# Gathering h for a graph attention layer: two tiles per chunk by column copies, and some tiles by single-row transfers

## The reference, cut to what matters

```
h = maximum(layernorm(x), 0)                       # 12500 nodes, 64 features
h_edge = ((h[src] + edge_attr) @ W)                # 200000 edges, sorted by dst, 2 heads of 64
s = leaky_relu(<h_edge, attn_l> + <h @ W, attn_r>[dst])
alpha = softmax of s over the edges of each dst
ft = segment_sum(h_edge * alpha, dst); mean over heads; batch norm; relu; + x
```

## Time and profile before

| | us |
|---|---|
| median of 3 runs (1983.07 to 1984.06) | 1983.39 |
| the profiled execution's own time | 1986.6 |
| span of the profiled execution | 1984.9 |
| POOL busy | 1469.0 (74%), 1558 instructions |
| DVE busy | 1141.2 (57%) |
| ACT busy | 413.0 (21%) |

### The profile page before, as it was taken

The page is one execution under the profiler, slowest core; times in us unless marked ns, Lnnn a source line. Parts: engine busy times, 40 slices in busy tenths (PEclk is TensorE's granted clock), DMA queues, the critical chain, the costliest instruction groups (busy, mean ns, idle before and its releaser), DMA issues.

```text
span 1984.9 us, 25091 instructions
## 1 busy us (share of the span) xinstructions
PE 925.4 (47%) x6252; PEld 662.5 (33%) x6252; DVE 1141.2 (57%) x3283; ACT 413.0 (21%) x2927; POOL 1469.0 (74%) x1558
## 2 busy tenths in 40 slices
PE   3537535433553445344534543554355435543555
PEld 2425323322332233233323332333233223332335
DVE  7878646555655465556545554555455546554665
ACT  3420111311131122112211221122113111211102
POOL 7777777777777777777777777777777777777771
PEclk9758767676676677667766766676667666766676
DMA  8734322232223222322232232223222322232235
GB/s 231 176 81 124 94 59 60 61 92 60 60 67 86 60 60 68 85 60 61 74 79 60 61 81 72 60 61 93 60 60 60 93 60 61 60 92 60 60 69 135
DMA packets 72959, 156.70 MB, mean 79 GB/s; under 512 B 28756, under 2 KB 33376, under 8 KB 66160
## 3 DMA queue, kind: packets, MB, share of 16 engines
q0 software_dynamic: 49536, 52.31, 15.7%
q1 hardware_dynamic: 22162, 99.02, 15.2%
q10 hardware_dynamic: 1112, 3.73, 0.7%
HBM read 143.71 MB, written 9.80 MB: 77 GB/s over the span
## 4 chain that ended last, share of the span: by engine, by line
POOL 68%; issue 22%; DVE 4%; PE 3%; DMA 2%; ACT 0%; ACTq 0%; DVEq 0%; SPq 0%; POOLq 0%
POOL work L681 67%; PE p_s L930 1%; DMA er_run<-er_tab,er_idx 1%; DMA acc<-in_x 1%; DMA h_tab<-acc 1%; PE po L1053 1%; PE pt L919 0%; POOL er_run L695 0%; DVE acc L1534 0%; DVE acc L1230 0%; DVE acc L1228 0%; DVE work L1222 0%; DVE scaled L1220 0%; PE pt L1112 0%; PE p_s L962 0%
## 5 line engine op out<-in xcount | busy, mean ns | idle before, releaser
L681 POOL DMA_INDIRECT work<-h_tab,srcI x1477 | 1398.0, 946 | 450.4 <-issue 450.1
L1178 DVE COPY elh<-work 128x16 f32<-128x16 f32 x196 | 38.7, 198 | 699.8 <-DMA work<-h_tab,srcI 697.8
L990 PE MATMUL p_s<-ident,elh 128*32 128x128 f32 x196 | 50.7, 412 | 746.8 <-DVE elh L1178 746.8
L825 ACT ACTIVATE cols<-acc 32x2 f32 x2688 | 298.9, 201 | 136.3 <-issue 136.3
L1053 PE MATMUL po<-scaled,work 128*65 128x64 f32 x3104 | 250.8, 257 | 77.6 <-issue 74.5
L990 PEld LDWEIGHTS p_s<-ident,elh 128*32 128x32 f32 x196 | 25.7, 155 | 758.0 <-DVE elh L1178 754.1
L1053 PEld LDWEIGHTS po<-scaled,work 128*65 128x65 f32 x3104 | 245.5, 173 | 87.8 <-issue 87.0
L838 ACT ACTIVATE fexp<-fdif 1x2 f32<-1x2 f32 x49 | 9.9, 203 | 1209.3 <-DVEq L1134 1209.3
L962 PE MATMUL p_s<-work,wpair 128*32 128x256 f32 x784 | 234.9, 466 | 14.5 <-DVE p_r L1452 12.9
L952 PE MATMUL pt<-ident,work 128*128 128x128 f32 x784 | 159.4, 356 | 62.2 <-DVE work L1183 61.5
L1534 DVE TENSOR_TENSOR acc<-acc,po 65x64 f32 x776 | 168.4, 217 | 27.7 <-DVE acc L1534 1.4
(11 more groups left out here) (214 smaller groups left out, 968.5 us busy)
## 6 DMA issues: line engine op xcount, KB each, us to landing
work<-in_ea_t SPq DMA_DIRECT2D x49, 1024.0 KB, 6.1
ohT_i<-in_dst_n SPq DMA_DIRECT2D x49, 512.0 KB
work<-h_tab,srcI POOLq DMA_INDIRECT x1477, 2.5
acc<-hT_tab SPq DMA_DIRECT2D x2, 1562.5 KB, 14.0
h_tab<-acc SPq DMA_DIRECT2D x1, 2887.5 KB
work<-in_x SPq DMA_DIRECT2D x1, 2800.0 KB
out<-work SPq DMA_DIRECT2D x5, 448.0 KB
acc<-in_x ACTq DMA_DIRECT2D x3, 672.0 KB
```

The costliest lines, as they stand in the source:

```text
L681: pool.indirect_dma_start(out=row, out_offset=None, in_=x if c < RAW else h_tab, in_offset=bass.IndirectOffsetOnAxis(ap=srcI[:, c, j, g:g ...
L825: copied = nc.scalar.activation(view(cols[0:HALF, n % COL_BUFS, 0, i:i + 1], [[P, H]]), view(acc[CP:P, 0, bass.ds(r, 1)], [[NACC, H]]), AC ...
L990: m = mm(sT_ps[:, j * P:(j + 1) * P], elh[:, c % 2, j, :, :].rearrange("p h g -> p (h g)"), ident[:, :], start=False, stop=True, skip_grou ...
```

## The change: what it does

- **Columns.** Every chunk from 5 to 48 has two column tiles, (0, 12) and (1, 12): 88 tiles in place of 21. Both are made within one `load_cols(c)`, for chunk c + 2. The numbers of the two tiles' nodes are packed into one word, so one register serves two copies: the low 14 bits by `%`, the high ones by `>>`.
- **Who copies.** ACT takes 7 of 8 batches of 16 registers, so 112 registers and 224 copies in a chunk. DVE takes the last 16 registers and 32 copies in a new `load_cols(c)` of its own, between `make_e(c + 1, 2)` and the sums of the other 8 groups.
- **Adding.** `add_cols` treats 256 columns in place of 128, and waits for both `cols_ok` and `cols_dve_ok`.
- **Rows.** `ROW_FIRST` is 6 and every second chunk has a row tile: 21 tiles of 128 rows (chunks 7, 9, ... 47) beside the 64 rows of the last chunk. SP's loop issues two batches of 16 rows before `load_dst(c)` and two after `load_bond(c + 1)`.

In the cut below the first `load_cols`, with `nc.scalar`, is ACT's; the second, with `v.tensor_copy`, is DVE's.

```diff
-ROW_FIRST = NCH - 1
+ROW_FIRST = 6
-BATCHES = (3, 2)
-ROW_SPAN, ROW_SHARE = 8, 5
+BATCHES = (2, 2)
+ROW_SPAN, ROW_SHARE = 2, 1
-COL_FIRST, COL_STEP = 7, 2
+COL_FIRST = 5
-COL_BATCH = 32
+COL_BATCH, COL_ACT = 16, 7
+HI = 14
+LOW = (1 << HI) - 1
 def col_tiles(c):
-    return [(0, COL_G)] if c >= COL_FIRST and (c - COL_FIRST) % COL_STEP == 0 and c < NCH - 1 else []
+    return [(j, COL_G) for j in range(EPP)] if c >= COL_FIRST else []
...
             def load_cols(c):
-                n, part = divmod(c - COL_FIRST + 1 + COL_STEP, COL_STEP)
...
+                n = c + 2 - COL_FIRST
+                if n < 0 or c + 2 >= NCH:
                     return
-                if n >= COL_BUFS and part == 0:
+                if n >= COL_BUFS:
                     act.wait_ge(cols_added, n - COL_BUFS + 1)
-                cc = COL_CHUNKS[n]
-                for r0 in range(part * COL_PART * COL_BATCH, (part + 1) * COL_PART * COL_BATCH, COL_BATCH):
-                    for i, r in enumerate(col_regs(cc, r0, r0 + COL_BATCH, ENG.Activation), r0):
-                        copied = nc.scalar.activation(view(cols[0:HALF, n % COL_BUFS, 0, i:i + 1], [[P, H]]),
-                                                      view(acc[CP:P, 0, bass.ds(r, 1)], [[NACC, H]]), ACT.Copy)
+                for r0 in range(0, COL_ACT * COL_BATCH, COL_BATCH):
+                    for i, r in enumerate(col_regs(c + 2, r0, r0 + COL_BATCH, ENG.Activation), r0):
+                        for to, node in ((i, r % (LOW + 1)), (P + i, r >> HI)):
+                            copied = nc.scalar.activation(view(cols[0:HALF, n % COL_BUFS, 0, to:to + 1], [[GROUP, H]]),
+                                                          view(accf[CP:P, bass.ds(node, 1)], [[NACC, H]]), ACT.Copy)
                     copied.then_inc(cols_ok, 1)
...
             def bond_scores(c):
                 if col_tiles(c):
-                    pe.wait_ge(cols_added, COL_CHUNKS.index(c) + 1)
+                    pe.wait_ge(cols_added, c - COL_FIRST + 1)
...
+            step(v.tensor_scalar(t[:, 0:P], node[:, P:EPP * P], HI, None, ALU.logical_shift_left))
+            step(v.tensor_tensor(node[:, 0:P], node[:, 0:P], t[:, 0:P], ALU.bitwise_or))
             signal(coffs_ok)
...
+            def load_cols(c):
+                n = c + 2 - COL_FIRST
+                if n < 0 or c + 2 >= NCH:
+                    return
...
+                if n >= COL_BUFS:
+                    dve.wait_ge(cols_added, n - COL_BUFS + 1)
+                for i, r in enumerate(col_regs(c + 2, COL_ACT * COL_BATCH, P, ENG.DVE), COL_ACT * COL_BATCH):
+                    for to, node in ((i, r % (LOW + 1)), (P + i, r >> HI)):
+                        copied = v.tensor_copy(view(cols[0:HALF, n % COL_BUFS, 0, to:to + 1], [[GROUP, H]]),
+                                               view(accf[CP:P, bass.ds(node, 1)], [[NACC, H]]))
+                copied.then_inc(cols_dve_ok, 1)
             def add_cols(c):
...
-                dve.wait_ge(cols_ok, (n + 1) * P // COL_BATCH)
+                dve.wait_ge(cols_ok, (n + 1) * COL_ACT)
+                dve.wait_ge(cols_dve_ok, n + 1)
                 step(v.tensor_copy(cols[HALF:F, n % COL_BUFS, 0, :], cols[0:HALF, n % COL_BUFS, 1, :]))
-                at = bt[c % 2][0:F, g // 2, j * P:(j + 1) * P]
+                at = bt[c % 2][0:F, COL_G // 2, :]
                 v.tensor_tensor(at, at, cols[0:F, n % COL_BUFS, 0, :], ALU.add).then_inc(cols_added, 1)
...
+                    if g0 == 0:
+                        load_cols(c)
```

More of the change, by code:

```diff
@@ L52 @@
 ROW_BUFS = 4
-ROW_FIRST = NCH - 1
+ROW_FIRST = 6
 BATCH = 16
-BATCHES = (3, 2)
-ROW_SPAN, ROW_SHARE = 8, 5
+BATCHES = (2, 2)
+ROW_SPAN, ROW_SHARE = 2, 1
 COL_G = 12
-COL_FIRST, COL_STEP = 7, 2
+COL_FIRST = 5
 COL_BUFS = 2
-COL_BATCH = 32
-COL_PART = P // COL_BATCH // COL_STEP
-assert COL_PART * COL_STEP * COL_BATCH == P and COL_G % 2 == 0
+COL_BATCH, COL_ACT = 16, 7
+assert COL_G % 2 == 0 and COL_BATCH * (COL_ACT + 1) == P
+HI = 14
+LOW = (1 << HI) - 1
+assert N <= LOW and LOW < H * NACC
 def col_tiles(c):
-    return [(0, COL_G)] if c >= COL_FIRST and (c - COL_FIRST) % COL_STEP == 0 and c < NCH - 1 else []
-COL_CHUNKS = [c for c in range(NCH) if col_tiles(c)]
+    return [(j, COL_G) for j in range(EPP)] if c >= COL_FIRST else []
 def row_tiles(c):
@@ L157, in gnn_kernel @@
         row_tile = sb("row_tile", [P, ROW_BUFS, FH])
-        cols = sb("cols", [P, 4, H, P])
+        cols = sb("cols", [P, COL_BUFS, H, GROUP])
         raw_mv = sb("raw_mv", [P, 2, EPP, CG])
@@ L321, in gnn_kernel @@
         cols_ok = sem("cols_ok")
+        cols_dve_ok = sem("cols_dve_ok")
         cols_added = sem("cols_added")
@@ L453, in col_regs @@
             return nc.values_load_multi_w_load_instructions(
-                coffs[c:c + 1, o0:o1], engines=[which], min_val=0, max_val=N - 1,
-                skip_runtime_bounds_check_because="src and dst hold numbers of nodes")[1]
+                coffs[c:c + 1, o0:o1], engines=[which], min_val=0, max_val=((N - 1) << HI) + LOW,
+                skip_runtime_bounds_check_because="each half of a word holds the column of a node, in [0, N)")[1]
         h_bytes = h_tab.rearrange("n f -> (n f)").bitcast(u8)
@@ L815, in load_cols @@
             def load_cols(c):
-                n, part = divmod(c - COL_FIRST + 1 + COL_STEP, COL_STEP)
-                if not 0 <= n < len(COL_CHUNKS):
+                n = c + 2 - COL_FIRST
+                if n < 0 or c + 2 >= NCH:
                     return
-                if n >= COL_BUFS and part == 0:
+                if n >= COL_BUFS:
                     act.wait_ge(cols_added, n - COL_BUFS + 1)
-                cc = COL_CHUNKS[n]
-                for r0 in range(part * COL_PART * COL_BATCH, (part + 1) * COL_PART * COL_BATCH, COL_BATCH):
-                    for i, r in enumerate(col_regs(cc, r0, r0 + COL_BATCH, ENG.Activation), r0):
-                        copied = nc.scalar.activation(view(cols[0:HALF, n % COL_BUFS, 0, i:i + 1], [[P, H]]),
-                                                      view(acc[CP:P, 0, bass.ds(r, 1)], [[NACC, H]]), ACT.Copy)
+                for r0 in range(0, COL_ACT * COL_BATCH, COL_BATCH):
[3 more added lines that the diff above has]
+                                                          view(accf[CP:P, bass.ds(node, 1)], [[NACC, H]]), ACT.Copy)
                     copied.then_inc(cols_ok, 1)
@@ L1420, in _ @@
             last_base = []
+            def load_cols(c):
+                n = c + 2 - COL_FIRST
+                if n < 0 or c + 2 >= NCH:
+                    return
+                if n == 0:
+                    dve.wait_ge(cols_table_in, 32)
+                if n >= COL_BUFS:
[5 more added lines that the diff above has]
+                copied.then_inc(cols_dve_ok, 1)
             def add_cols(c):
-                j, g = col_tiles(c)[0]
-                n = COL_CHUNKS.index(c)
+                n = c - COL_FIRST
                 dve.wait_ge(bt_in[c % 2], 16 * (c // 2 + 1))
-                dve.wait_ge(cols_ok, (n + 1) * P // COL_BATCH)
+                dve.wait_ge(cols_ok, (n + 1) * COL_ACT)
+                dve.wait_ge(cols_dve_ok, n + 1)
                 step(v.tensor_copy(cols[HALF:F, n % COL_BUFS, 0, :], cols[0:HALF, n % COL_BUFS, 1, :]))
-                at = bt[c % 2][0:F, g // 2, j * P:(j + 1) * P]
+                at = bt[c % 2][0:F, COL_G // 2, :]
                 v.tensor_tensor(at, at, cols[0:F, n % COL_BUFS, 0, :], ALU.add).then_inc(cols_added, 1)
```

## The result

| | before | after |
|---|---|---|
| median, 4 runs each | 1983.72 (1983.07 to 1984.43) | 2561.62 (2559.69 to 2563.42) |
| span of the profiled execution | 1984.9 | 2558.0 |

The ratio is 1.2915, with a 95% interval of 1.2899 to 1.2932: 29% slower. The forecast of 2700 is 5% too high, the range of 2370 to 2900 holds the time, and the side was right. Measured once more, beside another kernel, the changed kernel gave 1.2918 (1.2897 to 1.294).

A forecast was written before the change was run, and what follows sets the result against it. POOL's count of gathers bounds the kernel now; afterwards ACT's 45.3 us and DVE's 10.2 form a 55.5 us period. 199.9 us, 44 periods (2442) and 60.5 make a span of 2702, given as 2700; range 2370 to 2900.

The forecast's parts named there:

- The ring: From one `pT` to the next, DVE's first part and ACT's copies run one after the other: period 55.5 us.
- POOL: Gathers on POOL: 88 fewer, 1389 left, at 1.251 us each; 36.9 us a chunk, under the new period.
- ACT's stage: ACT's register loads and copies from the start of `pT`: 33.0 us plus 12.3 for taking numbers apart, 45.3 us.
- rest: On ACT, the start behind `pT`, the end of the last copy and stalls: 1.4 us a chunk.
- Unpacking: One `%` or `>>` added to each ACT copy: 0.055 us a copy, 12.3 us a chunk, bounds 0 and 0.12.
- the ring's DVE part: DVE from `add_cols` to `sdif`'s end, without the wait for gathered rows: 10.2 us a chunk.
- Is it hidden?: Added register work on ACT is not hidden: ACT idles 1.96 of a load's 1.98 us, so its queue is not ahead.
- Rival 1: Taking numbers apart on ACT nearly free, 0 to 0.03 us a copy: 2160 to 2455 us; chance 0.18.
- Rival 2: Taking numbers apart on ACT dear, 0.075 to 0.12 us a copy, or more stalls: 2900 to 3340 us; chance 0.12.
- Rival 3: POOL stays the bound, faster: 88 gathers saved, 110.1 us, so 1873; ACT's part at most 26.7 us; chance 0.03.
- Rival 4: SP as new bound: 26.3 us of rows a chunk plus waits; needs a period under about 30; no separate chance.
- DVE's own copies: DVE's 32 copies and their load between `sdif` and the chunk's end: 11.0 us, covered by ACT's 45.3, costing nothing.

The follow-up runs named there:

- opening the ring: Changed kernel with three column buffers in place of two and copies made for chunk c + 3: 2101.03 us, ratio 1.0598.
- row tiles alone: Kernel before with only the change's 21 row tiles and four batches of 16 rows a chunk, column tiles as before: 1956.66 us, ratio 0.9869.
- one column tile: Kernel before with the 21 row tiles and one unpacked column tile a chunk for chunks 5 to 47, copied by ACT: 1929.41 us, ratio 0.9733.
- the ring open and no unpacking: Changed kernel with one register a copy, three column buffers and copies made for chunk c + 3: 2000.86 us, ratio 1.0087.
- The column tiles alone: Changed kernel with the row-tile settings as before, so without its new row tiles: 2555.88 us, ratio 1.2888.
- the run with one register a copy: Changed kernel with numbers left unpacked, loads of 32 registers for 32 copies: 2461.38 us, ratio 1.2416.

## Why the prediction was right, step by step

**Where the bound goes.** Right. The ring of `add_cols`, `sdif`, `pT` and ACT's copies set the pace; the wait, its line and its releaser are as named, and opening the ring gave 461 us back.

**POOL.** Right: 1389 gathers, (1311.7 + 427.7) / 1389 = 1.252 us each, and 88 fewer are worth nothing in this kernel. Where POOL stays the bound, each gather less was worth 1.24 to 1.27 us (row tiles alone: 26.6 us for 21; one column tile: 53.1 for 43).

**ACT's stage**, forecast 45.3 us, measured 41.7:

| term | forecast | measured |
|---|---|---|
| 7 loads of 16 registers | 7.7 | 7 x 1.03 = 7.2 |
| 224 copies with unpacking | 23.9 + 12.3 = 36.2 | 224 x 0.147 = 32.9 |
| rest | 1.4 | 1.6 |

**Unpacking** is the term that was mis-sized: 0.055 us a copy was taken, nearly a whole instruction, and it is 0.040, since the operation rides in the instruction that is there. That is 224 x 0.015 = 3.4 us a chunk too much. The prediction took the value between bounds of 0 and 0.12 without a row that priced it, so being this near is partly luck. With the load's -0.5 and small ones of +0.2 and +0.3 (the ring's DVE part is 10.5, forecast 10.2) the period is 52.23 in place of 55.5, and 44 x 3.3 = 145 us is the whole miss of the span, forecast 2702: 200.3 + 44 x 52.23 + 59.5 = 2558.

**Is it hidden?** No, as argued. The engine still idles 1.02 of the 1.03 us of a load, so the queue is not ahead. The part of a copy's pace that is not the register instruction stayed the same, 107 - 46 = 61 and 147 - 85 = 62 ns: the two come one after the other.

**Rival 1** (unpacking nearly free, 2160 to 2455) fell, but not by much: 0.040 is near its bound of 0.03. The rule of the Trainium skill, "Advanced Engine Details and Errata", sections "Sequencer Loop" and "Engine Queue Depths", that a sequencer goes on while its engine's instructions wait, had nothing to hide here. With the register work hidden the time would have been 2160, and 2562 was measured: the copies' pace grew by the full 40 ns of the longer register instruction (0.107 to 0.147) and fell back with it. **Rival 2** (2900 to 3340) fell with the same 0.040. **Rival 3** (POOL stays the bound, 1873) needs ACT's stage at 26.7 us at most, and it was 41.7. Even with the ring open and no unpacking ACT's queue sets 39.1 us, above POOL's 36.9. **Rival 4**: SP's rows are hidden. SP's timeline in one chunk:

```profile
1040.56 24.98 SPq L564 DMA_DIRECT2D row_tile<-h_tab  x64
1065.59 0.37 SPq L521 DMA_DIRECT2D ohT_i<-in_dst_n  x1
```

Four batches take 1.2 + 25.0 us with their first load, as forecast (26.3). The dst numbers are loaded 27.1 us after `pT` (1065.59 - 1038.50), and 10.6 us after it in the run without the row tiles (1046.84 - 1036.21): 16.5 us of delay, where 13.2 were forecast, and DVE waits for none of these loads. What the rows do cost, 5.7 us, is DVE's, as shown under "The column tiles alone"; the prediction had left it out.

**DVE's own copies** were put at 11.0 us and took 1.36 + 5.63 = 7.0. They are hidden, and still hidden when doubled.

## What to carry to other kernels

When work moves to an idle engine, do not ask how idle it is but what it stands behind and who waits for its end. Here 62% busy on ACT and 54% on DVE made a kernel 29% slower, because each waited for the other once a chunk; one more buffer of lead gave 80% of it back. Then price the queue, not the engine: for copies of 64 numbers the register loads (7.2 us) and address instructions (224 x 0.085 = 19.0) are most of ACT's 41.7 us. With a lead of a whole chunk, a smaller share (1.5 column tiles), unpacked numbers and 26 row tiles the same idea became a gain of 4%.

## What the runs showed of the hardware

- On ACT a register instruction takes 46 ns with the address's three operations, 87 with `%` by 16384 added and 85 with `>>` by 14. On DVE it takes 57 with the three (in the run with one register a copy) and 108 in the median with the fourth. Whether another form of unpacking would be cheaper was not tried.
- A register load costs by the register and by the engine: 16 registers 1.03 us on ACT and 1.35 on DVE; 32 registers 1.98 on ACT and 2.37 on DVE.
- DVE's copies of 32 x 2 numbers came every (5.63 - 0.16) / 31 = 0.18 us, ACT's every 0.147, with the same unpacking: the difference of 0.03 is near that of the register instructions (0.108 - 0.085).
